# Second attention: one of four key groups with fp32 exponentials as the stationary operand

## The reference, cut to what matters

```python
B, S, D = x.shape                 # 16, 256, 128, after a layer norm
hd = D // H                       # H = 16 heads of 8
Hkv = H // G                      # 4 key/value groups, each shared by 4 heads
q, k, v = x @ Wq, x @ Wk, x @ Wv
...
q, k = _rope(q, ...), _rope(k, ...)
scores = jnp.einsum('bhqd,bhkd->bhqk', q, k) / jnp.sqrt(jnp.float32(D))
p = jax.nn.softmax(scores, axis=-1)        # over 256 keys, no mask
o = jnp.einsum('bhqk,bhkd->bhqd', p, v)
return o.transpose(0, 2, 1, 3).reshape(B, S, D) @ Wo
```

## Time and profile before

| | us |
|---|---|
| median of 3 runs | 1943.48 (1939.62 to 1945.4) |
| profiled execution, its own time | 1943.49 |
| its span | 1941.6 |
| PE busy, whole span | 1223.6 (63%) |
| DVE busy | 1135.1 (58%) |
| POOL busy | 966.6 (50%) |
| PEld busy | 904.9 (47%) |
| ACT busy | 782.2 (40%) |
| exponentials L1812, 128 | 142.7, mean 1.115 |
| roundings L1819, 128 | 135.5, mean 1.059 |
| subtractions on DVE L1884, 64 | 97.1, mean 1.517 |
| subtractions on POOL L1679, 64 | 151.3, mean 2.364 |
| row maxima L1908, 128 | 156.0, mean 1.219 |
| value products L1734, 1024 | 75.2, mean 0.179 |

### The profile page before, as it was taken

One profiled execution on the slowest core, in us unless ns is written; L12 is line 12 of the kernel. 1 busy time (PEld: TensorE's weight loads), 2 busy tenths in 40 slices (PEclk: granted clock), 3 DMA queues, 4 the chain that ended last, 5 costly groups with the idle time before them and its releaser, 6 DMA issues.

```text
span 1941.6 us, 34590 instructions
## 1 busy us (share of the span) xinstructions
PE 1223.6 (63%) x11544; PEld 904.9 (47%) x11545; DVE 1135.1 (58%) x2883; ACT 782.2 (40%) x1164; POOL 966.6 (50%) x1052
## 2 busy tenths in 40 slices
PE   2397587862981359779353578777762349678360
PEld 1297355551981128668321244444432129678320
DVE  6546667666468713225357699899978713225332
ACT  2153266650440114334111488788881114334110
POOL 0625145443241665535574467666740665535564
PEclk9998689985995589889776555555555679889785
DMA  8233044401220115345211000000000115345212
GB/s 336 66 96 103 18 155 148 139 15 37 87 82 14 41 46 179 130 137 167 83 49 35 13 2 2 2 2 2 2 2 1 43 58 177 122 147 160 78 49 76
DMA packets 99997, 150.42 MB, mean 77 GB/s; under 512 B 21408, under 2 KB 54816, under 8 KB 99104
## 3 DMA queue, kind: packets, MB, share of 16 engines
q1 hardware_dynamic: 79392, 106.76, 16.7%
q0 software_dynamic: 20480, 41.98, 7.4%
HBM read 74.16 MB, written 74.45 MB: 77 GB/s over the span
## 4 chain that ended last, share of the span: by engine, by line
POOL 24%; PE 23%; issue 16%; DMA 15%; DVE 14%; SPq 5%; ACT 2%; DVEq 0%; ACTq 0%; POOLq 0%
POOL slots_top L619 12%; POOL AREA L1075 11%; DMA slots_top<-XN,ROW 6%; DMA AREA<-results_top,ROW 5%; PE PS L841 4%; SPq L1274 3%; PE PS L293 2%; PE PS L295 2%; PE PS L294 2%; PE PS L1718 2%; DVE AREA L1884 2%; PE PS L1734 2%; PE PS L1706 2%; DMA query_rows<-AREA 1%; PE PS L412 1%
## 5 line engine op out<-in xcount | busy, mean ns | idle before, releaser
L619 POOL DMA_INDIRECT slots_top<-XN,ROW x320 | 315.0, 984 | 363.2 <-DVE ROW L573 183.8
L1075 POOL DMA_INDIRECT AREA<-results_top,ROW x320 | 305.2, 954 | 310.9 <-DMA results_top<-AREA 123.6
L990 DVE SCALAR_TENSOR_TENSOR AREA<-PS,AREA 128x512 f32<-128x512 f32 x96 | 66.4, 691 | 295.5 <-ACT AREA L969 295.0
L1679 POOL TENSOR_TENSOR AREA<-AREA 128x1024 f16<-128x1024 f32 x64 | 151.3, 2364 | 91.1 <-ACT AREA L1819 90.9
L902 PE MATMUL PS<-WGU,AREA 128*128 x768 | 189.5, 391 | 0.0
L1908 DVE TENSOR_REDUCE AREA<-PS 128x4 f32<-128x1024 f32 x128 | 156.0, 1219 | 30.1 <-PE PS L1706 29.3
L1812 ACT ACTIVATE AREA<-PS,AREA 128x1024 f32<-128x1024 f32 x128 | 142.7, 1115 | 52.6 <-PE PS L1718 52.4
L902 PEld LDWEIGHTS PS<-WGU,AREA 128*128 128x128 f32 x768 | 144.0, 198 | 17.1 <-ACT AREA L959 0.4
L1307 POOL TENSOR_TENSOR AREA<-AREA 128x1536 f16<-128x1536 f32 x32 | 92.9, 2904 | 98.4 <-ACT AREA L1522 98.4
L1819 ACT ACTIVATE AREA<-AREA 128x1024 f16<-128x1024 f32 x128 | 135.5, 1059 | 0.0
L412 PE MATMUL PS<-IDF,XN 128*128 128x128 f32 x192 | 50.4, 422 | 135.0 <-DVE XN L402 135.0
(11 more groups left out here) (260 smaller groups left out, 3558.9 us busy)
## 6 DMA issues: line engine op xcount, KB each, us to landing
AREA<-slots_top SPq DMA_DIRECT2D x96, 256.0 KB, 3.0
results_top<-AREA SPq DMA_DIRECT2D x96, 256.0 KB, 2.1
slots_top<-ZERO SPq DMA_DIRECT2D x24, 512.0 KB, 3.1
AREA<-slots_top SPq DMA_DIRECT2D x48, 128.0 KB, 2.3
results_top<-AREA SPq DMA_DIRECT2D x48, 128.0 KB, 1.7
AREA<-query_rows SPq DMA_DIRECT2D x48, 128.0 KB, 2.9
slots_top<-XN,ROW POOLq DMA_INDIRECT x320, 2.2
AREA<-results_top,ROW POOLq DMA_INDIRECT x320
```

The source lines that it names most:

```text
L619: nc.gpsimd.indirect_dma_start(out=L.xs[q], out_offset=bass.IndirectOffsetOnAxis(ap=ROW[:, n:n + 1], axis=0), in_=XN[:, t * D:(t + 1) * D] ...
L1075: nc.gpsimd.indirect_dma_start(out=YG[:, at:at + D], out_offset=None, in_=L.ys[g * GT // L.tiles], in_offset=bass.IndirectOffsetOnAxis(ap= ...
L1679: nc.gpsimd.tensor_tensor(PB1[1][:, g, :], PF1[:, g, :], PB1[0][:, g, :], ALU.subtract).then_inc(b_plo[1].sem, 1)
```

## The change

Group 0 is no longer split. Its exponentials stay in PF1 in fp32, and its value products take them as the stationary operand in fp32, 8 products for a tile (4 heads, 2 key blocks) instead of 16. The moving operand is a new fp32 buffer VF with 17 columns for each tile: 8 values, a one, and 8 zeros, which ACT fills from the projection with one more copy for each tile, and POOL sets up with two memsets. `phi` and `plo` of group 0 go away on ACT and DVE. PB1 has 3 slots instead of 4. Group 0's products wait for the exponential of group 0 instead of the subtraction, and the next tile's exponential of group 0 waits for these products. Groups 1 to 3 stay as they are, with their counts renumbered.

```diff
         VP = area([NT, 68], F16)
+        VF = area([NT, 17], F32)
...
-        PB1 = [area([4, 1024], F16) for _ in range(2)]
+        PB1 = [area([3, 1024], F16) for _ in range(2)]
...
         def wait_split(eng, i, c, g):
 
-            wait(eng, b_plo[g % 2], 2 * (i * 8 + c) + g // 2 + 1)
+            t = i * 8 + c
+            wait(eng, b_plo[g % 2], 2 * t + g // 2 + 1 if g % 2 else t + 1)
...
             nc.gpsimd.memset(ones, 1.0).then_inc(b_cst.sem, 1)
-            pool.wait_ge(*b_cst.at(7))
+            nc.gpsimd.memset(VF[:, :, 9:17], 0.0).then_inc(b_cst.sem, 1)
+            nc.gpsimd.memset(VF[:, :, 8], 1.0).then_inc(b_cst.sem, 1)
+            pool.wait_ge(*b_cst.at(9))
...
             def values(i, c, g):
                 t = i * 8 + c
-                wait_split(pe, i, c, g)
                 if g == 0:
+                    wait(pe, b_exp, 4 * t + 1)
                     wait(pe, b_oc, t)
+                else:
+                    wait_split(pe, i, c, g)
                 for r in range(4):
                     o = (4 * g + r) * 17
                     for k in range(2):
+                        if g == 0:
+                            v = VF[:, bass.ds(i * 8 + c // 2 * 2 + k, 1), :].rearrange("p a c -> p (a c)")
+                            at = (r % 2 * 4 + k * 2 + r // 2) * P
+                            ins = nc.tensor.matmul(banks(6)[:, o:o + 17], PF1[:, 0, at:at + P], v, start=k == 0,
+                                                   stop=k == 1)
+                            continue
...
             def exp(i, c, g):
                 n = 4 * (i * 8 + c) + g
                 wait(act, b_st, n + 1)
-                if tile_exists(i, c - 1):
+                if tile_exists(i, c - 1) and g == 0:
+                    wait(act, b_pv, n - 3)
+                elif tile_exists(i, c - 1):
                     wait_split(act, i, c - 1, g)
...
                         wait(act, b_proj, t + 6)
+                        nc.scalar.activation(VF[:, bass.ds(t + 5, 1), 0:8].rearrange("p t c -> p (t c)"),
+                                             banks(0)[:, 320:328], ACT.Copy, scale=1.0 / SW)
...
                     before = c - 1 if g < 1 else c
-                    if tile_exists(i, before):
+                    if tile_exists(i, before) and g != 1:
                         phi(i, before, (g - 1) % 4)
...
-                    if g == 1 and tile_exists(i, c):
-                        plo(i, c, 0)
```

More of the change, by code:

```diff
@@ L1647, in attn1_pool @@
             nc.gpsimd.memset(ones, 1.0).then_inc(b_cst.sem, 1)
-            pool.wait_ge(*b_cst.at(7))
+            nc.gpsimd.memset(VF[:, :, 9:17], 0.0).then_inc(b_cst.sem, 1)
+            nc.gpsimd.memset(VF[:, :, 8], 1.0).then_inc(b_cst.sem, 1)
+            pool.wait_ge(*b_cst.at(9))
             nc.gpsimd.memset(KP[:, :, :, 24], MSCALE).then_inc(b_cst.sem, 1)
-            pool.wait_ge(*b_cst.at(8))
+            pool.wait_ge(*b_cst.at(10))
             def pack_k(i, c):
@@ L1677, in plo @@
             def plo(i, c, g):
-                wait(pool, b_phi, 4 * (i * 8 + c) + g + 1)
-                nc.gpsimd.tensor_tensor(PB1[1][:, g, :], PF1[:, g, :], PB1[0][:, g, :],
+                wait(pool, b_phi, 3 * (i * 8 + c) + g)
+                nc.gpsimd.tensor_tensor(PB1[1][:, g - 1, :], PF1[:, g, :], PB1[0][:, g - 1, :],
                                         ALU.subtract).then_inc(b_plo[1].sem, 1)
@@ L1694, in attn1_tensor @@
             pe.wait_ge(*b_wlo.at(2))
-            pe.wait_ge(*b_cst.at(8))
+            pe.wait_ge(*b_cst.at(10))
             pe.wait_ge(*ln_xt.at(NG))
@@ L1730, in values @@
                     for k in range(2):
+                        if g == 0:
[4 more added lines that the diff above has]
+                            continue
                         v = VP[:, bass.ds(i * 8 + c // 2 * 2 + k, 1), g * 17:(g + 1) * 17].rearrange("p a c -> p (a c)")
                         at = (r % 2 * 4 + k * 2 + r // 2) * P
-                        p = [PB1[n][:, g, at:at + P] for n in range(2)]
+                        p = [PB1[n][:, g - 1, at:at + P] for n in range(2)]
                         nc.tensor.matmul(banks(6)[:, o:o + 17], p[0], v, start=k == 0, stop=False)
@@ L1804, in attn1_scalar @@
                 nc.scalar.activation(w[0][:, :], WST[:, c:c + m], ACT.Copy, scale=SW).then_inc(b_whi.sem, 1)
-            act.wait_ge(*b_cst.at(8))
+            act.wait_ge(*b_cst.at(10))
             def exp(i, c, g):
@@ L1818, in phi @@
                 wait(act, b_pv, n - 3)
-                nc.scalar.activation(PB1[0][:, g, :], PF1[:, g, :], ACT.Copy).then_inc(b_phi.sem, 1)
+                nc.scalar.activation(PB1[0][:, g - 1, :], PF1[:, g, :], ACT.Copy).then_inc(b_phi.sem, 1)
             def turn(i, c):
@@ L1860, in attn1_vector @@
                                                op0=ALU.mult, op1=ALU.subtract).then_inc(b_wlo.sem, 1)
-            dve.wait_ge(*b_cst.at(8))
+            dve.wait_ge(*b_cst.at(10))
             def rope(i, c):
@@ L1882, in plo @@
             def plo(i, c, g):
-                wait(dve, b_phi, 4 * (i * 8 + c) + g + 1)
-                nc.vector.tensor_tensor(PB1[1][:, g, :], PF1[:, g, :], PB1[0][:, g, :],
+                wait(dve, b_phi, 3 * (i * 8 + c) + g)
+                nc.vector.tensor_tensor(PB1[1][:, g - 1, :], PF1[:, g, :], PB1[0][:, g - 1, :],
                                         ALU.subtract).then_inc(b_plo[0].sem, 1)
@@ L1943, in attn1_vector @@
                 statistics(NT - 1)
-        ATTN1_COUNTS = {b_w: 64, b_cst: 8, b_whi: 2, b_wlo: 2, b_pack_k: NT, b_pstep: 2 * NT}
+        ATTN1_COUNTS = {b_w: 64, b_cst: 10, b_whi: 2, b_wlo: 2, b_pack_k: NT, b_pstep: 2 * NT}
         ATTN1_COUNTS.update({s: NT for s in (b_proj, b_rope, b_vhi, b_vlo, b_pack, b_ktr, b_kt, b_q1tr, b_q1, b_m,
@@ L1948, in build @@
                                              b_nstep, b_rstep)})
-        ATTN1_COUNTS.update({s: 4 * NT for s in (b_s, b_max, b_st, b_exp, b_phi, b_pv)})
-        ATTN1_COUNTS.update({s: 2 * NT for s in b_plo})
+        ATTN1_COUNTS.update({s: 4 * NT for s in (b_s, b_max, b_st, b_exp, b_pv)})
+        ATTN1_COUNTS.update({b_phi: 3 * NT, b_plo[0]: NT, b_plo[1]: 2 * NT})
         def moe_counts(L):
```

## The result

The changed kernel took 2030.26 us (median of 4 runs, 2025.44 to 2032.05) against 1941.55 us for the kernel before in the same series. The ratio is 1.0451, with a 95% interval of 1.0433 to 1.047. The difference is 88.7 us. Forecast were 2033 us, in a range of 2023 to 2042.

What follows compares the result with a forecast made beforehand. A circle of waits PE, DVE, PE, ACT was taken to bound the kernel, with a DVE path within 0.1 us. 89.4 + 2.4 + 1 + 0.7 - 1 - 3 = 89.5 on 1943.49 gave 2033 us, range 2023 to 2042.

Steps and rivals of the forecast that it cites:

- products, turns 1 to 30: Group 0's value products on PE: fp32 in place of fp16 adds 2.98 us a tile, 89.4 us in all.
- loop jumps: Second attention's two jumps back: PE's longer product stream may hide them, 0 to -6 us, taken as -3.
- turn 0: First turn, no output copy to wait for: longer products delay the next maximum on DVE, +2.4 us.
- turn 31 and drain: Last turn: late output product delays DVE's residual addition and group 2's subtraction, so the last products end later, +1 us.
- filling, fp32 copy: ACT's added fp32 value copy delays rotation only while the pipeline fills: 5 turns x 0.15, +0.7 us, bounds 0 and +1.
- removed work: Group 0's rounding on ACT and subtraction on DVE go away: at most DVE's near-tie goes, -1 us, bounds 0 and -3.
- The circle: Chain of waits PE, DVE, PE, ACT sets the 11.06 us turn; group 0's products lie on it, all 2.98 us added.
- The price of a pass: Each fp32 product on PE is two passes of 213 ns, set by the weight load; 17 moving columns change nothing.
- A second path within 0.1 us: DVE's run through rotation and normalisation to the next maximum, almost as long as the circle; freeing it gives 0.1 us a turn.
- The clock: PE's granted clock stays at 0.50; rival of a full rise: 1891 us, chance 3%; half way: 1962, 3%.
- POOL's subtraction: POOL's group 3 subtraction, for which PE sometimes waits, stays near 2.75 us without DVE's subtraction beside it: 0 gain.
- What would show it: Signs: loads 213 ns apart, output copies every 14.0 us, clock 0.50, DVE idle ahead of L1908 up 3 us a turn.

Runs made afterwards that it cites:

- experiments 1 and 2: Kernel before plus fp32 products, rounding and subtraction kept: 2023.68 us, ratio 1.042; changed kernel with fp16 products, no fp32 value copy, rounding and subtraction removed: 1941.54 us, 1.0002.
- experiment 7: Changed kernel with 4 of group 0's 8 fp32 products a tile, waits kept: 2045.08 us beside 2012.16, ratio 1.0158.
- experiment 6: Changed kernel with 64 moving columns instead of 17 in each fp32 product of group 0: 2099.61 us, ratio 1.0436.
- experiment 10: Changed kernel, ACT's output copy ahead of group 3's exponential, DVE's group 2 subtraction at the end of the turn before: 1962.53 us, ratio 1.0118.
- experiment 8: Kernel before, ACT's output copy ahead of group 3's exponential, DVE's group 2 subtraction at the end of the turn before: 2012.51 us, ratio 0.9994.
- experiment 11: Kernel before with only ACT's output copy moved ahead of group 3's exponential: 1978.96 us, ratio 1.0203.

## Why the prediction was right, point by point

| Step | Predicted, us | Measured, us | From |
|---|---|---|---|
| products, turns 1 to 30 | 89.4 | 89.35 | 415.03 - 331.68 between the copies of turns 1 and 31, and the jumps' 6.0 added back |
| loop jumps | -3 (0 to -6) | -6.0 | 6.5 over the usual turn before, 0.5 after |
| turn 0 | +2.4 | +2.3 | first exponential to first copy, 17.49 and 19.76 |
| turn 31 and drain | +1 | +1.6 | last copy to statistics, 10.25 and 11.88 |
| filling, fp32 copy | +0.7 | +0.1 | first value copy (now the fp32 one) to first exponential, 24.40 and 24.54 |
| removed work | -1 (0 to -3) | +1.6 to +1.7, most of it inside the first line | experiments 1 and 2 |
| sum | 89.5 | 87.4 | |

The rest of the profiled execution was 5 us shorter than before, in phases where nothing was changed, and the medians are 88.7 apart. That the first line agrees to 0.05 us is luck: the stream grew by 2.94 us on the mean of the two kinds of turn, not by the 2.98 read from one of them, and the removed work added 0.08 us a turn; in the last turns, behind the loop, the difference was mostly smaller. So is part of the closeness of the whole: three more us gained at the jumps stand against 2.6 lost on the removed work. The prediction's range is also looser at its lower end than its terms: jumps hidden, DVE's path freed and no filling cost take 5.7 us off 2033 (3, 2 and 0.7), not 9, which gives 2027. The measured median lies above that too.

- **The circle.** It was right that group 0's products lie on the path that sets the turn and that nothing covers them. Experiment 7 shows it by dose: 1.71 us less stream, 1.71 us less turn.
- **The price of a pass.** 213 ns from L1232 became 213 to 214. The load sets it, not the moving columns: experiment 6 put 47 columns more into every pass and paid for them once. The Trainium skill ("TensorE: Matmul & The Clock Gate", section LDWEIGHTS) gives a weight load in ns as its columns over 1.2, 107 ns for 128. This does not hold here for fp32: the measured pace is twice that. By an estimate from that rule the change would have cost 40 us.
- **The removed work.** The sign was wrong and the size small. A second path within 0.1 us had been counted as worth 1 us; no gain from it shows, and ACT's wait came out 0.08 us a turn dearer.
- **The jumps.** The step could go from 0 to -6 and the end was left open; it is -6. The longer the stream that the array still works on, the less of the jump is left: 0.43, 1.71 and 3.43 us of stream in the kernel before, in experiment 7 and in the changed kernel. The prediction's own check, PE's "issue" below 1 us, holds: after the changed kernel's first jump the next scores start 0.5 us after the output product.

```profile
1244.81 0.27 PE L294 MATMUL PS<-AREA 128*128 128x128 f16 x1
...
1245.33 0.61 PE L1722 MATMUL PS<-AREA 32*128 32x256 f16 x4
```

- **The clock.** It did not rise: it is 0.50 in the stage of every variant, with 64 columns as with 17, and in experiment 10 with PE busy 98%.
- **POOL's subtraction.** 2.76 us, as predicted from the earlier trace rows.
- **What would show it.** The prediction had DVE's idle time ahead of the maximum L1908 up by 3 us a turn. It went up by 4.4 us in all, from 0.9 to 5.3: the 3 us by which the turn grew, and the work that went away. Only 2.1 us of that stand ahead of the maxima (now L1924); 2.3 us are ahead of the residual addition (now L1952) and end with the output product.

## What to carry to other kernels

Price a product by its stationary operand when its moving side is short: going from split fp16 to fp32 halved the number of products here and made their time seven to eight times as long. Before work is taken from the busiest engine, follow one turn around: an engine that is 92% busy gave nothing back, because the path ran through a wait on another one. Where a short instruction of DVE ends just ahead of a long one of POOL (0.24 us here), any reordering, also one that removes a wait, has to be checked against who now starts first.

## What the runs showed of the hardware

- An fp32 product with 128x128 stationary and 17, 32 or 64 moving columns is two passes of 213 to 214 ns at the lower clock; an fp16 one with 17 or 9 takes 27 to 33 ns (16 in 0.43 or 0.53 us). 47 more moving columns cost 0.08 us for 16 passes, at the two ends of the stream (experiment 6).
- A jump of the hardware loop costs PE about 3.7 us (an estimate: stream and extra added), less what the array still has to do: extras of 3.2 and 3.3, 1.9 and 2.1, 0.26 and 0.23 us behind streams of 0.43, 1.71 and 3.43 us. How much of it reaches the turn depends on the waits that follow: with other orders and a stream as short as before, the extras were 1.8 and 1.4 us (experiment 8) and none (experiment 11). Turns inside the loop are 0.09 us (before) and 0.22 us (changed) longer than the same turns written out.
- A DVE instruction of 0.28 us with two SBUF inputs took 2.10 us when it started 0.04 us after a POOL subtraction of 2.00 us, and 0.96 us when it met the end of one. The Trainium skill ("SBUF — State Buffer", section "SBUF: two separate sides") says that DVE, where it reads two SBUF inputs, and GpSimd share a port pair that whoever starts first keeps for the whole instruction; this trace agrees for POOL first. It agrees the other way too: POOL's subtraction takes 2.75 us where DVE's began 0.33 us before it, and 2.00 us in most other places.
- The granted clock stayed at 0.50, the 1.2 GHz level, in this stage of every kernel looked at, while PE's busy share went from 77% (184.56 of the 240 us from 1200 to 1440) before to 83% (200.34) in the changed kernel and 98% (235.30) in experiment 10.
